# Front of a graph, attention and expert layer: TensorE fillers, small VectorE forms, load order, place of two products and of a search

## The reference

```python
def _L0_gnn_ref(x, rots, idx_i, idx_j):      # m: 100,000 plane rotations one after another, out of range indices dropped
    m = _build_mat(rots, idx_i, idx_j, x.shape[-1])
    return x @ m

def _L0_mix_ref(feature, W_qk, b_qk, W_v, b_v, gamma, beta):
    QK = einsum('bnd,kde->bkne', feature, W_qk) + b_qk
    value = einsum('bnd,de->bne', feature, W_v) + b_v
    query = QK[:, 0]; key = QK[:, 1]
    sm = softmax(key, axis=1)                      # over the 6250 rows
    lam = einsum('bnd,bne->bde', sm, value)
    bn = (lam - mean) * rsqrt(var + BN_EPS) * gamma + beta
    return einsum('bnd,bde->bne', query, bn)

xn = _layernorm(x)
x = x + _L0_gnn_ref(xn, edge_weight, src, dst) + _L0_mix_ref(xn[None], ...)[0]
x = x + _L0_ffn_ref(_layernorm(x)[None], ...)[0]   # 8 experts, top 2, gelu
```

## Time and profile before

| | us |
|---|---|
| median of 3 runs | 1029.9 (1027.6 to 1032.25) |
| the profiled execution | 1028.55 |
| its span, first to last instruction | 1026.7 |
| around the span (start and end) | 1.85 |
| TensorE busy, share of the span | 939.8, 92% |
| VectorE busy | 725.3, 71% |
| ScalarE busy | 667.0, 65% |
| GpSimd busy | 593.5, 58% |
| TensorE's first product of the loop of groups | at 146.41 |

### The profile page before, as it was taken

The page is one execution under the profiler, slowest core; times in us unless marked ns, Lnnn a source line. Parts: engine busy times, 40 slices in busy tenths (PEclk is TensorE's granted clock), DMA queues, the critical chain, the costliest instruction groups (busy, mean ns, idle before and its releaser), DMA issues.

```text
span 1026.7 us, 26096 instructions
## 1 busy us (share of the span) xinstructions
PE 939.8 (92%) x6344; PEld 821.0 (80%) x6345; DVE 725.3 (71%) x2604; ACT 667.0 (65%) x1906; POOL 593.5 (58%) x927
## 2 busy tenths in 40 slices
PE   6899979899999999999998729999999989999997
PEld 4557758788888888888775419999989979999997
DVE  5965579789999889988768844444444447777775
ACT  6578747677777777776438736666656646666664
POOL 7813675566666566666426744666643246666664
PEclk8989999999999999999999959999999989999999
DMA  8323116611010000122115643444422223333332
GB/s 255 81 72 95 26 27 213 183 17 17 17 28 21 17 17 17 22 25 19 18 63 183 201 137 102 143 120 127 119 86 66 69 73 101 105 99 98 108 106 67
DMA packets 64684, 86.19 MB, mean 84 GB/s; under 512 B 18148, under 2 KB 52930, under 8 KB 64386
## 3 DMA queue, kind: packets, MB, share of 16 engines
q1 hardware_dynamic: 44879, 43.17, 15.2%
q0 software_dynamic: 19184, 42.04, 14.7%
q10 hardware_dynamic: 576, 0.54, 0.2%
HBM read 54.18 MB, written 33.02 MB: 85 GB/s over the span
## 4 chain that ended last, share of the span: by engine, by line
PE 55%; DVE 9%; issue 8%; DMA 5%; POOL 4%; ACT 3%; DVEq 1%; SPq 0%; POOLq 0%; ACTq 0%
PE banks L1920 16%; PE banks L1930 16%; PE banks L1744 5%; PE banks L1686 4%; PE banks L1755 4%; PE banks L1696 4%; DMA R<-incl_d,R 3%; POOL send_d L669 3%; PE banks L1911 2%; ACT R L759 2%; PE banks L1872 1%; PE banks L1727 1%; DVE R L1199 1%; DVE R L1172 1%; DVE Mrot L1254 1%
## 5 line engine op out<-in xcount | busy, mean ns | idle before, releaser
L1920 PE MATMUL banks<-R 128*128 128x128 f32 x1696 | 210.7, 278 | 2.4 <-ACT R L995 2.4
L1920 PEld LDWEIGHTS banks<-R 128*128 128x128 f32 x1696 | 201.5, 195 | 3.0 <-ACT R L995 2.9
L1930 PE MATMUL banks<-R 128*128 x848 | 201.4, 381 | 0.0
L1008 ACT ACTIVATE R<-banks,b1c 128x128 f32<-128x128 f32 x424 | 143.3, 365 | 52.4 <-PE banks L1920 50.6
L1930 PEld LDWEIGHTS banks<-R 128*128 128x128 f32 x848 | 153.9, 191 | 16.7
L995 ACT ACTIVATE R<-banks,bet_c,gam_c 128x128 f32<-128x128 f32 x212 | 85.6, 454 | 106.0 <-PE banks L1911 102.4
L1526 DVE COPY R<-R 128x1024 f32 x106 | 74.1, 700 | 76.7 <-PE banks L1920 60.8
L669 POOL DMA_INDIRECT send_d<-R,slot_all x98 | 95.9, 979 | 50.7 <-issue 42.8
L682 POOL DMA_INDIRECT first_d<-R,dest_now x54 | 58.9, 1090 | 96.9 <-DVE R L1531 87.7
L1744 PEld LDWEIGHTS banks<-R 128*128 128x128 f32 x768 | 95.6, 191 | 17.3 <-ACT R L891 15.7
L1744 PE MATMUL banks<-R 128*128 128x126 f32 (+5 forms) x768 | 104.3, 279 | 4.6 <-ACT R L891 4.6
(11 more groups left out here) (323 smaller groups left out, 1922.9 us busy)
## 6 DMA issues: line engine op xcount, KB each, us to landing
R<-send_d SPq DMA_DIRECT2D x106, 131.0 KB
R<-in_L_ffn_W_dram SPq DMA_DIRECT2D x16, 512.0 KB
R<-in_x_dram SPq DMA_DIRECT2D x14, 512.0 KB, 4.8
R<-in_x_dram SPq DMA_DIRECT2D x5, 1024.0 KB, 11.0
rec_d<-R SPq DMA_DIRECT2D x1, 2800.0 KB
send_d<-zrow SPq DMA_DIRECT2D x14, 131.0 KB, 5.9
send_d<-R,slot_all POOLq DMA_INDIRECT x98
R<-incl_d,R POOLq DMA_INDIRECT x80
```

Source lines behind the costliest of these rows:

```text
L1008: last = nc.scalar.activation(hT[b][:, c, :], bank[2 + 2 * b + c // 2][:, (c % 2) * P:(c % 2 + 1) * P], ACT.Gelu, bias=b1c[:, bass.ds(e, 1 ...
L1920: last = mm(bank[2 + 2 * b + c // 2][:, (c % 2) * P:(c % 2 + 1) * P], w1c[b][:, kb, c * P:(c + 1) * P], xmT[b][:, kb * P:(kb + 1) * P], st ...
L1930: last = mm(bank[6 + b][:, 0:D], hT[b][:, c, :], w2s[:, bass.ds(e, 1), c, :].rearrange("p a h -> p (a h)"), start=(c == 0), stop=(c == H / ...
```

## The change

In the front, seven things are edited:

1. The tail of x is loaded as 96 and 10 rows, the edge arrays as 112 and 13 partitions each (six issues on GpSimd's queue for three), with the counts of the waits changed to suit.
2. The first four tiles of x are issued ahead of `wk`.
3. Two of GpSimd's tensor_scalar operations (L540) clamp with minimum before maximum, where the maximum came first.
4. ScalarE's last `search_in(2)` stands behind `exps(12)`; `search(3)` is now directly ahead of it.
5. VectorE's small tensor_tensor and tensor_copy operations on 128x2 tiles are written as scalar_tensor_tensor.
6. `totals()` stands behind `turn_in(5)` in step 3, where it stood behind `turn_exps(3)`.
7. Eight products `ident` by `ident` into `misc` stand ahead of `turn_exps` in each of steps 0 to 3.

```diff
@@ -369,13 +369,14 @@
             def load_x(i):
                 c = 8 * i
                 if i == 2:
-                    sp.wait_ge(S["edges"], 48)
+                    sp.wait_ge(S["edges"], 96)
                 sp.dma_start(x_all[:, c:c + 8, :], xg_src[:, c:c + 8, :]).then_inc(S[f"xld{i}"], 16)
             def load_half(half):
                 sp.dma_start(x_all[:, 4 * half:4 * half + 4, :], xg_src[:, 4 * half:4 * half + 4, :]).then_inc(S["xld0" + "ab"[half]], 16)
-            sp.dma_start(x_all[0:TAIL, FULL, :], x[FULL * P:N, :]).then_inc(S["xld_tail"], 16)
+            for r0, r1 in ((0, TAIL - TAIL % 16), (TAIL - TAIL % 16, TAIL)):
+                sp.dma_start(x_all[r0:r1, FULL, :], x[FULL * P + r0:FULL * P + r1, :]).then_inc(S["xld_tail"], 16)
+            load_half(0)
             sp.dma_start(wk, W_qk[1].rearrange("(k p) e -> p k e", p=P)).then_inc(S["keys_loaded"], 16)
-            load_half(0)
             with nc.allow_non_contiguous_dma(reason="one column of a small vector"):
                 sp.dma_start(bk_c[:, :], b_qk[1].rearrange("(k p) -> p k", p=P)).then_inc(S["bias_k"], 16)
             load_half(1)
@@ -505,7 +506,8 @@
             for c in (2, 4, 5):
                 link(nc.gpsimd.memset(padd[:, c:c + 1], -1.0))
             for dstt, s in ((i_raw, src), (j_raw, dst), (theta, edge_weight)):
-                nc.gpsimd.dma_start(dstt, s.rearrange("(p l) -> p l", p=EP)).then_inc(S["edges"], 16)
+                for into, out_of in zip(parts_of(dstt), parts_of(s.rearrange("(p l) -> p l", p=EP))):
+                    nc.gpsimd.dma_start(into, out_of).then_inc(S["edges"], 16)
             pool.wait_ge(S["consts"], 1)
             link(nc.gpsimd.tensor_copy(identb[:, :], ident[:, :]))
             link(nc.gpsimd.memset(tri[:, :], 0.0))
@@ -532,12 +534,12 @@
 
 
             link(nc.gpsimd.memset(rec[:, :, 2], 0.0))
-            pool.wait_ge(S["edges"], 48)
+            pool.wait_ge(S["edges"], 96)
             link(TSp(i_f, i_raw, 0.5, 0.5, ALU.mult, ALU.add))
             link(TSp(j_f, j_raw, 0.5, 0.5, ALU.mult, ALU.add))
             for free, end in ((g_i, i_f), (g_j, j_f)):
                 link(TSp(free, end, -4.0, 2.0 * D + 2.0, ALU.mult, ALU.add))
-                link(TSp(free, free, 0.0, 2.0, ALU.max, ALU.min))
+                link(TSp(free, free, 2.0, 0.0, ALU.min, ALU.max))
             TTp(cnt, g_i, g_j, ALU.add).then_inc(S["cnt_ready"], 1)
             link(TSp(rec[:, :, 6], g_i, 1.0, -1.0, ALU.mult, ALU.add))
             link(TTp(g_i, j_f, i_f, ALU.subtract))
@@ -863,9 +865,9 @@
             start_step(10)
             search(2, range(G))
             end_step(10)
-            search_in(2, range(G))
             search(3, range(G))
             exps(NG12)
+            search_in(2, range(G))
 
 
             act.wait_ge(S["ngroups"], 1)
@@ -1051,7 +1053,7 @@
 
             def tail_stats():
 
-                dve.wait_ge(S["xld_tail"], 16)
+                dve.wait_ge(S["xld_tail"], 32)
                 own(nc.vector.bn_stats(stats[0:TAIL, FULL, :], x_all[0:TAIL, FULL, :]))
                 return nc.vector.bn_aggr(mv[0:TAIL, FULL, :], stats[0:TAIL, FULL, :])
 
@@ -1082,13 +1084,13 @@
                 last.then_inc(S["dve"], 1)
                 dve.wait_ge(S["dve"], n0 + 1)
                 at_least(dve, S["exp_done"], q)
-                TT(new_m[:, :], run_m[:, :], grp_m[:, :], ALU.max).then_inc(S["dve"], 1)
+                STT(new_m[:, :], run_m[:, :], 1.0, grp_m[:, :], ALU.mult, ALU.max).then_inc(S["dve"], 1)
                 dve.wait_ge(S["dve"], n0 + 2)
-                TT(dm[:, :], run_m[:, :], new_m[:, :], ALU.subtract)
-                TT(ebias[:, :], bk_c[:, :], new_m[:, :], ALU.subtract).then_inc(S["dve"], 1)
+                STT(dm[:, :], run_m[:, :], 1.0, new_m[:, :], ALU.mult, ALU.subtract)
+                STT(ebias[:, :], bk_c[:, :], 1.0, new_m[:, :], ALU.mult, ALU.subtract).then_inc(S["dve"], 1)
                 dve.wait_ge(S["dve"], n0 + 3)
-                TT(ebias[:, :], ebias[:, :], bk_c[:, :], ALU.subtract).then_inc(S["ebias_ready"], 1)
-                nc.vector.tensor_copy(run_m[:, :], new_m[:, :])
+                STT(ebias[:, :], ebias[:, :], 1.0, bk_c[:, :], ALU.mult, ALU.subtract).then_inc(S["ebias_ready"], 1)
+                STT(run_m[:, :], new_m[:, :], 1.0, new_m[:, :], ALU.mult, ALU.max)
 
             def turned_exps(q):
                 W = width(q)
@@ -1099,10 +1101,10 @@
                                                  bank[4 + kb][0:r, 0:nt * P].rearrange("p (t d) -> p t d", d=P))
                 last.then_inc(S["exT_done"], 1)
 
-                TT(ssum[:, :], ssum[:, :], alpha[:, :], ALU.mult).then_inc(S["dve"], 1)
+                STT(ssum[:, :], ssum[:, :], 1.0, alpha[:, :], ALU.mult, ALU.mult).then_inc(S["dve"], 1)
                 dve.wait_ge(S["dve"], q * PERM + (base + 4))
-                TT(ssum[:, :], ssum[:, :], gsum[:, :], ALU.add)
-                nc.vector.tensor_copy(alpha2[:, :], alpha[:, :]).then_inc(S["dve"], 1)
+                STT(ssum[:, :], ssum[:, :], 1.0, gsum[:, :], ALU.mult, ALU.add)
+                STT(alpha2[:, :], alpha[:, :], 1.0, alpha[:, :], ALU.mult, ALU.max).then_inc(S["dve"], 1)
                 dve.wait_ge(S["dve"], q * PERM + (base + 5))
 
             def weighted_sum(q):
@@ -1648,16 +1650,21 @@
 
             def mix_step(q, b):
                 const = isinstance(q, int)
+                if const and q < 4:
+                    constants(8)
                 turn_exps(q)
-                if const and q == 3:
-                    totals()
                 if not const or q + 1 <= NG12:
                     keys(q + 1)
                 if not const or q + 2 <= NG12:
                     turn_in(q + 2, (b + 2) % 3)
+                if const and q == 3:
+                    totals()
                 weigh(q, b)
-            for _ in range(12):
-                mm(misc[:, 0:P], ident[:, :], ident[:, :], start=True, stop=True)
+            def constants(n):
+
+                for _ in range(n):
+                    mm(misc[:, 0:P], ident[:, :], ident[:, :], start=True, stop=True)
+            constants(12)
             turn_in(0, 0)
             pe.wait_ge(S["keys_loaded"], 16)
             keys(0)
```

## The result

| | before | changed |
|---|---|---|
| median of 16 runs each, us | 1029.9 (1027.5 to 1035.5) | 1025.5 (1023.9 to 1029.9) |
| ratio, 95% interval | | 0.9967 [0.9956, 0.9979] |
| profiled execution, us (span) | 1028.55 (1026.7) | 1023.97 (1022.1) |
| mean granted clock | 0.969 | 0.978 |

By the ratio the change brings 3.4 us, between 2.2 and 4.5: the right sign, under half of the 7.6 us forecast. The medians differ by 4.4; the ratio comes from runs that stood side by side.

What follows compares the result with a forecast made beforehand. The front was taken as a ring whose slowest link changes, with TensorE at its end waiting for exponentials and its clock falling. Terms summed to -7.5 us, 7.6 with rounding: 1029.9 to 1022.3 us, range 1019 to 1027.5.

Steps and rivals of the forecast that it cites:

- 0 on the path: GpSimd's faster clamps: GpSimd gains 4.1 us but then waits for step 3's offsets, so the time changes by 0.
- The new form: VectorE's small operations as scalar_tensor_tensor do not wait for GpSimd; worth next to nothing on top of the products.
- the first rival: The new VectorE form waits for GpSimd too, +1.9 us in step 1, giving 1024.2 us; chance 0.17.
- Step 1, -1.7 forecast: Products fill the 2.37 us wait, the clock stays up, keys(2) takes 3.60 for 4.97 us; 0.3 of wait goes too.
- its net of -0.7: Step 0: eight products delay turn_exps(0) by 0.7 us, but keys(1) at full clock gains 1.4.
- the second rival: The clock falls anyway, as products hold it less well; keys(4) stays at 6.67 us, giving 1026.0 us; chance 0.15.
- Loads, -0.7: Start of the front: first tiles pass wk, turn_in(1) ends near 14.2 us; GpSimd's three more issues cost nothing.
- Steps 2 and 3, +0.7: Exponentials come 1.6 and 1.7 us earlier, but eight products stand there: +0.1 in step 2, +0.6 in step 3.
- Totals and the clock, -1.2 and -3.1: Step 3: the 1.21 us wait for the scan goes, and keys(4) at full clock takes 3.60 for 6.67 us.
- Last search, -1.5: End of the front: 0.9 us of the 3.14 us wait ahead of turn_exps(12), plus 0.6 in weigh(12).
- the third that I gave, 0.6 us: weigh(12), slowed by the clock, regains a third of 1.66 us, with 0 and 1.7 as ends.
- Later stages "shifted unchanged": Everything behind the front, the loop of groups included, starts earlier by the front's gain and takes as long as before.

Runs made afterwards that it cites:

- u_forms: Changed kernel with VectorE's eight small operations as tensor_tensor and tensor_copy again; 1024.7 us, ratio 0.9965 to the kernel before.
- after_again: The changed kernel unaltered, measured a second time, on a chip where every kernel took 7% longer; ratio 0.9984 to the kernel before.
- u_products: Changed kernel without the blocks of eight products ahead of turn_exps in steps 0 to 3; 1025.9 us, ratio 0.9967 to the kernel before.
- u_totals: Changed kernel with totals() behind turn_exps(3) again, ahead of keys(4); 1025.0 us, ratio 0.9971 to the kernel before.
- u_loads: Changed kernel with loads as before: tail and edge arrays unsplit, wk ahead of the first tiles; 1023.5 us, ratio 0.9954 to the kernel before.
- u_search: Changed kernel with search_in(2) ahead of search(3) and the last exponentials again; 1026.9 us, ratio 0.9990 to the kernel before.
- o_clamps: Kernel before with only the clamps' faster order; 1024.2 us, ratio 0.9947 to the kernel before, and 0.9970 when repeated on a slower chip.

## Why the prediction was wrong

The loss lies ahead of `turn_exps(4)`, and in step 1 above all. The sum stood at -2.4 us at the end of step 1; measured at the end of `keys(2)` are +3.9 (36.6 for 32.7). From there on the terms came out about as forecast or better. Three things that the prediction had wrong meet in step 1: the clamps at 0, a form that does not wait, and loads of which I had looked at the first tiles only. Their shares of the missing time are not parted by any run.

- **The clamps, "0 on the path"**: the first failing step. I wrote that the faster clamps move GpSimd's work 4 us forward "beside other VectorE operations" and priced that at nothing. It moved 1.4 us, which brings tensor_tensor L543 and the 1.62 us tensor_scalar L544 beside `maxima(1)`, where they hold two operations for 0.45 and 1.21 us. And a clamp that lets VectorE's two-input operations through in all but its first 0.87 us when slow holds one for its whole length when fast (`alpha2` at 23.38 beside 23.34 to 24.19). Undone in the changed kernel, 2.8 and 3.6 us. With the old loads it is 2.6 us at `turn_exps(4)` and nothing in the time, and on the kernel before the fast clamps alone went with a lower time. So the waits are shown, and what they cost in the end is not, beyond the changed kernel.
- **The new form.** I took it as free from one overlap, and the trace of u_forms refutes that: the forms' own worth on top of the products is zero, as the sum had it, but for a reason that was wrong, and the first rival, with its wait of 1.9 us in step 1, was the right case. It said 1024.2, measured were 1025.5. In the four operations of rows 5 both tensors were in SBUF, so by the rule they should have waited too. But GpSimd's tensor_scalar there, bfloat16 out of float32, was a slow one, 1.78 us for 256 columns where the fast ones take 0.86 for 800, and they met it 1.33 us after its start; that pair was no evidence for this one. The Trainium skill's rule ("SBUF — State Buffer", section "Who interferes with whom") held here for tensor_tensor and scalar_tensor_tensor beside fast instructions (up to 1.9 us for 0.16) and for a one-input tensor_scalar, which never took over 0.22 us. It did not hold beside the slow clamp behind its first 0.87 us, though that reads SBUF too: `dm` at 24.44 took 0.16 us within 22.72 to 25.60. By the rule's letter the clamps would have been an edit that only helps.
- **Step 1, -1.7 forecast (the sum to -2.4)**: +3.0 at `turn_exps(1)`, and `keys(2)` took 5.36 us, the clock down at 28 us. A wait of 2.37 us was to be filled; it grew to 1.95 of products and 3.95 of waiting. Step 0 did better than its net of -0.7: `turn_exps(0)` +0.2, `keys(1)` 3.60 for 5.05, together -1.5 at its end. In after_again `keys(1)` took 4.82, so the size was partly luck. I also read the first twelve products' 5.12 us as the low clock; the granted clock there is 1.00 from 2 to 7 us. What made them slow no run shows, and the second rival loses its argument "for it".
- **Loads, -0.7**: the first tiles came 3.1 us earlier and those of step 1, of which I said nothing, 1.2 us later. The edge data, whose three more issues I had put at nothing, came 2.7 us later. Worth nothing measurable.
- **Steps 2 and 3, +0.7**: +1.5 and +0.5 at `turn_exps(2)` and `(3)`. Of the +1.5, 0.9 is the low clock of step 1, so +1.1 is these steps' own. The longest stalls ahead of `turn_exps(2)` are 1.86 (at 35.66) and 1.55 us where there was one of 1.75.
- **Totals and the clock, -1.2 and -3.1**: between `turn_exps(3)` and `(4)` the changed kernel gains 4.9 us, so the size was right, but not the owner. u_products and u_totals both keep `keys(4)` at 3.6 to 3.7 us, and so do u_loads, u_search and o_clamps; with totals and search alone it takes 4.14. It was long only in the two profiles of the kernel before (6.67 and 5.41). So these 3 us are to be had once, by whichever edit, and I take that for the main reason why the gains do not add; no run isolates it.
- **Last search, -1.5**: 2.8 us at `turn_exps(12)`, 2.4 at the loop's start, 2.4 by the ratios. The mechanism was right: VectorE's `weighted_sum` was late next, and `weigh(12)` starts 0.8 us earlier (0.9 forecast). The rest is luck: `weigh(12)` ran at the full clock behind the one long wait of 3.33 us (3.72 us for 5.28). Of the fifteen profiles with the search moved only this one and u_forms show that; in the other thirteen it takes 5.12 to 6.61 us, in after_again 5.41. In the five with the old place it takes 5.28 to 6.77. With 3.72 and 5.41 us in the changed kernel's two profiles, the third that I gave, 0.6 us, is not refuted.
- **Later stages "shifted unchanged"**: nearly, in the mean. In single profiles they scatter, see below.
- **Open**: why the clamps alone, on the kernel before, gave 5.5 and 3.3 us while their loop starts 1.7 us later and 0.9 earlier. And what share the loads and the clamps each have in the 3.7 us that the whole change lacks against totals and search alone: the undone pairs overlap within their intervals, and the two edits work on each other, as the clamps' 4.1 us and the edge data's 2.7 set together what GpSimd does beside step 1.

## What to carry to other kernels

Before an operation on one of VectorE and GpSimd is made faster, lay the two timelines on each other at the new starts: what matters is which two-input operations then meet, and a slow operation may be the one that lets others pass. The cure for such a wait is not another form with two tensors but one whose second operand is a scalar per partition, and only in the steps where the engine has time for it; here it took the waits away, and its worth in the time stayed inside the intervals. A gain that hangs on the clock was had here once, by any of several edits, and in some places by chance of the one profile. Summed over edits that each remove the same fall it is counted several times, so try the edits apart before they are put together.
